# Attention scores made with keys on partitions, seeded with the row minimum, instead of turned probabilities

## What is computed

```
xn  = layernorm(x)
qg, k, v = split(xn @ w_qkv.T);  q, gate = split(qg)
q, k = rope(layernorm(q)), rope(layernorm(k))
scores = q k^T / sqrt(128), causal                  # 16 heads, 2048 x 2048
out = softmax(scores) @ v                           # a key head serves 4 query heads
out = (out * sigmoid(gate)) @ w_o.T
moe = sum over the 2 best experts of p_e * (relu(xn @ w_fc[e])**2 @ w_proj[e])
result = x + out + moe
```

## Time and profile before

| | |
|---|---|
| time, median of 3 runs | 1535.22 us (1534.33 to 1535.95) |
| span of the profiled execution | 1534.4 us, 29715 instructions |
| busy TensorE | 1501.5 us (98%) |
| busy TensorE weight loads | 1380.6 us (90%) |
| busy VectorE | 1304.1 us (85%) |
| busy ScalarE | 1152.4 us (75%) |
| busy GpSimd | 364.7 us (24%) |

### The profile page before, as it was taken

The page is one execution under the profiler, slowest core; times in us unless marked ns, Lnnn a source line. Parts: engine busy times, 40 slices in busy tenths (PEclk is TensorE's granted clock), DMA queues, the critical chain, the costliest instruction groups (busy, mean ns, idle before and its releaser), DMA issues.

```text
span 1534.4 us, 29715 instructions
## 1 busy us (share of the span) xinstructions
PE 1501.5 (98%) x10589; PEld 1380.6 (90%) x10589; DVE 1304.1 (85%) x3037; ACT 1152.4 (75%) x3017; POOL 364.7 (24%) x502
## 2 busy tenths in 40 slices
PE   5999999999999999999999999999999999999998
PEld 3889999999989999999998999999999899999998
DVE  8999888888998888788799888877879888887788
ACT  4777776778887778777878777777787877768765
POOL 6545434420322111111042211111104221011010
PEclk8999999999999999999999999999999999999999
DMA  5411011011121111111111110111022211001013
GB/s 175 163 38 46 28 43 51 30 53 49 60 60 49 35 42 49 39 39 39 59 59 59 40 49 12 49 39 39 20 74 63 60 49 42 18 22 31 9 50 124
DMA packets 45124, 78.82 MB, mean 51 GB/s; under 512 B 4784, under 2 KB 30896, under 8 KB 44784
## 3 DMA queue, kind: packets, MB, share of 16 engines
q1 hardware_dynamic: 41232, 66.65, 14.2%
q0 software_dynamic: 3744, 10.26, 1.9%
HBM read 58.25 MB, written 24.72 MB: 54 GB/s over the span
## 4 chain that ended last, share of the span: by engine, by line
PE 86%; DVE 8%; ACT 3%; issue 2%; DMA 1%; POOL 1%; SPq 0%; DVEq 0%; ACTq 0%; POOLq 0%
PE bank L1392 45%; PE o_bank L1392 22%; PE pt_bank L1467 14%; PE bank L1445 2%; PE bank L1488 2%; DVE t_same L1266 1%; DVE pT_lo L1316 1%; ACT probs L1017 1%; DVE bank L1299 1%; DVE t_same L1262 1%; ACT pT_hi L1036 1%; DVE neg_chunk_max L1302 1%; DVE sumsq L1234 1%; DVE t_same L1250 1%; PE bank L1509 1%
## 5 line engine op out<-in xcount | busy, mean ns | idle before, releaser
L1017 ACT ACTIVATE probs<-bank,neg_max 128x512 f32<-128x512 f32 (+3 forms) x640 | 400.0, 635 | 100.8 <-DVE neg_max L1309 61.5
L1316 DVE TENSOR_TENSOR pT_lo<-pt_bank,pT_hi 128x512 fp32r<-128x512 f32 (+1 forms) x576 | 369.5, 655 | 87.4 <-ACT pT_hi L1036 82.9
L1036 ACT ACTIVATE pT_hi<-pt_bank 128x512 fp32r<-128x512 f32 (+1 forms) x576 | 326.7, 579 | 119.7 <-PE o_bank L1392 59.3
L1392 PE MATMUL o_bank<-pT_hi,v_hi 128*128 128x256 f32 x1088 | 331.8, 305 | 0.4 <-DVE pT_lo L1316 0.3
L1467 PE MATMUL pt_bank<-ident_rows,probs 128*128 128x128 f32 x2176 | 313.3, 273 | 2.5 <-DVE pT_lo L1316 1.5
L1392 PE MATMUL o_bank<-pT_hi,v_lo 128*128 128x256 f32 x1088 | 307.2, 282 | 0.0
L1392 PE MATMUL o_bank<-pT_lo,v_hi 128*128 128x256 f32 x1088 | 306.6, 282 | 0.0
L1302 DVE TENSOR_REDUCE neg_chunk_max<-bank 128x1 f32<-128x512 f32 (+1 forms) x384 | 244.8, 651 | 58.7 <-PE bank L1392 58.1
L1467 PEld LDWEIGHTS pt_bank<-ident_rows,probs 128*128 128x128 f32 x2176 | 252.1, 140 | 25.2 <-DVE pT_lo L1316 3.8
L1392 PE MATMUL bank<-kT_hi,qT_hi 128*128 128x512 f32 (+3 forms) x640 | 242.7, 379 | 0.7 <-ACT probs L1017 0.6
L1392 PE MATMUL bank<-kT_hi,qT_lo 128*128 128x512 f32 (+3 forms) x640 | 231.2, 361 | 0.0
(11 more groups left out here) (167 smaller groups left out, 2852.1 us busy)
## 6 DMA issues: line engine op xcount, KB each, us to landing
norm_rows<-kept_tables SPq DMA_DIRECT2D x24, 384.0 KB, 3.1
made_tables<-kept_tables SPq DMA_DIRECT2D x24, 384.0 KB, 3.0
kept_tables<-made_tables SPq DMA_DIRECT2D x16, 384.0 KB, 2.5
rows<-xs SPq DMA_DIRECT2D x23, 258.0 KB, 2.7
expert_raw<-in_w_fc SPq DMA_DIRECT2D x23, 256.0 KB, 3.0
expert_raw<-in_w_proj SPq DMA_DIRECT2D x23, 256.0 KB, 2.7
xs<-in_x_fill SPq DMA_DIRECT2D x11, 516.0 KB, 5.4
w_raw<-in_w_in SPq DMA_DIRECT2D x7, 640.0 KB, 4.2
```

What stands on the lines that cost most here:

```text
L1017: act.activation(probs[:, u, h % 2, first:first + width], bank("scores", g, t, h, c)[:, 0:width], ACT.Exp, bias=neg_max[:, u, h % 2:h % 2 ...
L1036: act.activation(pT_hi[:, n % PT_RING, 0:width], pt_bank[n % 2][:, 0:width], ACT.Copy)\
L1316: dve.tensor_tensor(pT_lo[:, n % PT_RING, 0:width], pt_bank[n % 2][:, 0:width], pT_hi[:, n % PT_RING, 0:width].bitcast(F32), ALU.subtract) ...
L1392: ins = pe.matmul(out_ap, s, m, start=(start and done == 1), stop=(stop and done == last))
```

## The change

The scores are now made with the keys on partitions, so that the exponentials come out as the value product needs them and nothing is turned.

- A softmax needs the row extreme before the exponential. It now comes from a one-pass product of the hi parts alone: `A` (PE, one matmul in place of three, queries on partitions), then `max` as before, and `min` over the chunks where there are several. The 128 x 4 result `row_min` is stored to memory (`mu_store`) and loaded back spread over all partitions (`mu_load`) as `min_rows`, 128 x 512: query and head in the columns.
- For each block j of 128 keys: `seed` (ScalarE, Copy with scale -1) writes the negated `min_rows`, or for the diagonal block `masked_min` (made by GpSimd, `masked`), into one of two banks `st_bank`. `st` adds the three-pass product of key block and 512 query columns on top (no matmul of it starts a group). `exp` writes `pT_raw` in SBUF, a ring of three; `p_hi` and `p_lo` now read `pT_raw`, and `pv` takes 512 columns at once. One `bits` step at the start puts the two banks into the state in which matmuls add.
- The accumulator of `exp` can't give row sums now. GpSimd adds the blocks up element by element, `psum`, one instruction of 128 x 512 for each block but the first of a tile (484 in all), into `lane_sum`. `SUMT` turns it, `sums` reduces it on VectorE, and the inverse goes out to memory and back (`inv_store`, `inv_load`); only in the last tile it is turned by TensorE (`INVB`).
- The gate projection is made turned, 128 features by 512 tokens, for four tiles at once (`G`, 64 steps as before). `gate_scale` and `GT` are gone. `og0` (VectorE) multiplies gate and `o_bank` in place of `o_take` and `og`; the product with the inverse sum, `og`, is GpSimd's (63 instructions of 128 x 512).
- The seven other banks: two for `st_bank` (before: `pt_bank`), five general ones, now free for any step. `BEGIN` and `DUE` have new values. qT, oT are now double buffers.

The core of the diff:

```diff
+ST_BANKS = 2
+RAW_RING = 3
@@ program_steps
-                    add("pe S", ("scores", g, t, h, c), SCORE_US[w], [("k_lo", g, t)],
-                        b + DUE["scores"])
+                    add("pe A", ("A", g, t, h, c), APPROX_US[w], [("k_hi", g, t)], at)
+            for j in range(t + 1):
...
+                add("act seed", ("seed", g, t, j), 0.48, [("mu_load", g, t), ("masked", g, t) if j == t else None,
+                    back("exp", ST_BANKS), ("bits",)], at + DUE["seed"])
+                add("pe S", ("st", g, t, j), 0.695, [("seed", g, t, j), ("k_lo", g, t)], at)
+                freed = [back("p_lo", RAW_RING)]
...
+                    freed.append(("psum", g0, t0, 1 if t0 and not j0 else j0))
+                add("act S", ("exp", g, t, j), 0.5, [("st", g, t, j)] + freed, at + DUE["exp"])
+                add("act PT", ("p_hi", g, t, j), 0.5, [("exp", g, t, j), back("pv", PT_RING)], at + DUE["p_hi"])
+                add("dve PT", ("p_lo", g, t, j), 0.6, [("p_hi", g, t, j)], at + DUE["p_lo"])
@@ GpSimd
+                    else:
+                        w.wait_ge(summed, number[step] - 1)
+                        pool.tensor_tensor(total, pT_raw[:, (m - 1) % RAW_RING] if j == 1 else total, pT_raw[:, m % RAW_RING],
+                                           ALU.add).then_inc(summed, 1)
+                elif kind == "og":
...
+                    pool.tensor_tensor(oT[:, t % 2], oT[:, t % 2], inv_rows[:, t % 2], ALU.mult).then_inc(og_done, 1)
@@ ScalarE
-                    act.activation(probs[:, u, h % 2, first:first + width],
-                                   bank("scores", g, t, h, c)[:, 0:width], ACT.Exp, bias=neg_max[:, u, h % 2:h % 2 + 1], scale=-1.0,
-                                   accum_out=chunk_sum[:, t % 2, h, c:c + 1]).then_inc(exp_done, 1)
+                    if m >= RAW_RING:
+
+                        w.wait_ge(pt_lo_done, m - RAW_RING + 1)
+                        w.wait_ge(summed, raw_freed(m - RAW_RING))
+                    act.activation(pT_raw[:, m % RAW_RING], st_bank[m % ST_BANKS][:], ACT.Exp, scale=-1.0).then_inc(exp_done, 1)
@@ VectorE
-                    dve.tensor_tensor(pT_lo[:, n % PT_RING, 0:width], pt_bank[n % 2][:, 0:width],
-                                      pT_hi[:, n % PT_RING, 0:width].bitcast(F32), ALU.subtract).then_inc(pt_lo_done, 1)
+                    dve.tensor_tensor(pT_lo[:, m % PT_RING], pT_raw[:, m % RAW_RING], pT_hi[:, m % PT_RING].bitcast(F32),
+                                      ALU.subtract).then_inc(pt_lo_done, 1)
@@ TensorE
+                    w.wait_ge(seeded, m + 1)
+                    three(st_bank[m % ST_BANKS][:], [(kT_hi[:, keys], kT_lo[:, keys])], [(qT_hi[:, t % 2], qT_lo[:, t % 2])],
+                          start=False, seeded_bank=True).then_inc(st_filled, 1)
```

583 lines of the change are left out of this document (316 added, 267 removed), and 27 rows, old and new, of the table BEGIN.

## The result

The changed kernel takes **2312.05 us** (median, 2309.49 to 2314.26), the kernel before 1534.80 beside it: 1.506 times as long, 95% interval 1.504 to 1.509. The forecast was 1587 us, with a range up to 1690. The direction was right, the size was not: 725 us are missing from the sum. The kernels of experiments 1 and 8 were timed four times, the others once; executions of one kernel lie within 6 us of each other.

The account below looks back on a forecast made before the run. TensorE's stream of products bound the kernel before; after the change VectorE would, with 1320 us of own load, 220 of port waits and idle of 9, 7 and 30, span 1586: forecast 1587 us, range 1425 to 1690.

Parts of the forecast that it names:

- between ... I allow 2%, 30 us: VectorE idle between start and end of the span, also for short tiles where the minimum goes through memory: 30 us.
- The wait at the port: VectorE instructions with two SBUF inputs wait for GpSimd's SBUF-reading products: 0.36 us for each of 611, 220 us.
- its own load: VectorE's busy time without port waits: 1304 + 13, about 1320 us, 93% of TensorE's 1413.
- the likeliest case: VectorE held up at the port: 1587 us, own range 1520 to 1680, chance 0.57.
- how long does VectorE wait for one GpSimd product?: Port step: at least 0, at most 1.06 us; by chance order 0.32 + 0.04 = 0.36 us.
- 46 us of idle: Idle on top of VectorE's 1540: 9 us at the start, 7 at the end, 30 between; span 1586.
- the floor of 1413: TensorE alone after a net 121 us less: 1534 - 121 = 1413 us, the ceiling of the gain.
- Ports meet rarely: Rival: block sums fall beside VectorE's reductions and gaps, waits under 0.1 us each; 1425 us, chance 0.23.
- Two banks: Rival: seed, products, exponential through two score banks cost 0.2 us on each of 364 blocks; about 1490 us, chance 0.11.
- GpSimd behind: Rival: late GpSimd sums hold everybody through the ring of three `pT_raw`, 2 us a tile; 1715 us, chance 0.09.
- Doesn't keep the products together: Rival: 512-column value products no cheaper than two of 256, TensorE losing only 9 us; inside the range, no chance given.
- The marks: Signs of being right: `pT_lo` 0.9 us or more, VectorE over 95%, TensorE under 93%, GpSimd's 512-wide products 1.4 or more.

Follow-up runs that it names:

- experiment 1: Changed kernel without either trip through memory: TensorE turns spread row minima and inverse sums, VectorE multiplies by the inverse; 1836.99 us, 1.197 times the kernel before.
- Experiment 8: Kernel of experiment 1 with the exponential written over the scores in PSUM, both parts split from there, GpSimd summing the high parts, three score banks; 1805.06 us.
- experiment 4: Changed kernel with both stores as 128 rows of 16 bytes in place of 512 single floats, both trips and the order kept; 1848.12 us.
- experiment 9: Kernel of Experiment 8 with each GpSimd block sum replaced by three fills of together 1.3 us; 1617.80 us.
- Experiments 7 and 12: 7: kernel of experiment 1, each GpSimd block sum replaced by three fills, 1588.50 us; 12: kernel before, 512 times four GpSimd fills added, 1640.28 us.
- the nearest, at 1577: Kernel of experiment 1 with each GpSimd block sum replaced by one fill of the same 512 columns; 1576.51 us.

## Why the prediction was wrong

**The trips through memory: the step that failed.** The prediction put them into "between ... I allow 2%, 30 us", with "a transfer of 384 KB lands after 3.0 us; here two in a row, behind others on SyncE". The forecast charged the trip to the short tiles; the trace has the seeds wait for it 52 times, up to 15.9 us, in all parts of the span. Two things were wrong. The row is of a transfer in long pieces, and the new stores are in pieces of 4 bytes, which the diff says in so many words (`allow_slow_non_contiguous=True`, "h q -> q h"); they land after 9.1 us. And the wait was not multiplied: the two trips take 9.1 + 4.6 + 9.0 + 4.8 = 27.5 us for each of 64 tiles, of which the span has 36.1 each, and SyncE stands 15.8 of them, with everything behind it. No row of before has such a store, so the term needed both bounds, as the port got, and had one. Measured: 464 us by experiment 4 (475 by experiment 1) in place of part of 30. That alone is 60% of the 777, and added to the forecast it goes beyond the range.

**The wait at the port: right mechanism, a term too small.** Forecast 0.36 us for each of 611 products, 220 us on VectorE. Experiment 4 has the changed kernel's instructions and order without the long stores, and VectorE is busy 1705 us there against its own load of 1320 as forecast, so 385, or 0.63 each. (That load is borne out within 2%: 1387 less 43 for the moved products, 1344, in experiment 9, where little is held.) In the changed kernel itself, where everything stands more, it is 1625 less 1320, 305. The 385 are within the bounds of 0 and 648, but their 0.63 is above the 0.5 a product at which the likeliest case ended. What failed is "how long does VectorE wait for one GpSimd product?": I asked it for each product of GpSimd, took chance order, and let at most one instruction of VectorE wait, once. Two rows of experiment 1 say otherwise. Products of the rope come five in a row just when GpSimd, after `rstd`, works off its sums without a gap, and one may wait for two. On the rope's 320 products alone VectorE spent 107 us more in experiment 1 (121.1 + 75.4 against 89.8), on the low parts about 140.

**What follows the wait.** I turned VectorE's load into time by adding 46 us of idle. In experiment 4 it was 141 (1846 less 1705): 1320 + 385 + 141 = 1846, where I had 1320 + 220 + 46 = 1586. These 260 us and the 464 of the stores are the whole miss, and 1848 lies outside the range already, so the second error alone would have failed the forecast too. That the idle comes by way of the rope is in part argued: TensorE waits there 131 us for `t_same`, VectorE's own idle is spread over many waits. Experiment 8 speaks for it from the other side: 131 us less of VectorE's low parts gave 32, or 61 with banks and order made equal.

The Trainium skill, SBUF — State Buffer, Who interferes with whom, was cited for this contention. It says that a VectorE instruction with two SBUF inputs contends with a GpSimd instruction that reads SBUF, not with one that only writes it. Experiments 7 and 12 agree (386 and 349 ns beside fills, 668 and 454 beside reading). Who comes second is blocked in full by that section; read as one instruction's wait at most, as the prediction read it, this is too little, by the 3343 ns above.

**TensorE.** The pitch of the 512-column value product was to be 0.232; in experiment 1 three follow from 1600.39 to 1600.86, 0.235 each. With the port out of the way its busy time is 1481 us against 1501 before. That is a gain of 21 where I had 121 and the turns of minima and inverse sums take some 56 back; busy time includes the overlap of products that wait, so the rest isn't settled. No run came near the floor of 1413; the nearest, at 1577, has TensorE at 94% and VectorE at 90%.

**The clock.** In the changed kernel the mean granted clock is 0.853 of 2.4 GHz with TensorE busy 71%, without trips 0.952 with 86%, with the fills 0.996 with 93%, as in the kernel before. Its products got longer with it: the first score product of a block means 483 ns in the changed kernel and 435 in experiment 1. The prediction had no word on it. I take it for a consequence of TensorE's standing; what the lower clock adds to the time no run separates.

**GpSimd and ScalarE.** GpSimd's 512-column product was to be 1.23 us and takes 1.27 undisturbed; busy 1115 forecast, 1272 measured. ScalarE 1210 forecast, 1242 measured.

**The rivals.** *Ports meet rarely* is refuted by the low part's 933 ns. *Two banks*: TensorE does wait 341 us for the seeds (its weight loads 388), as that rival would have it, but the seeds wait for the minima from memory, not for `exp`; without the trips TensorE's wait for seeds is 23 us. *GpSimd behind*: `exp` waits 77 us for scores, 55 for `pT_lo` and only 14 for `lane_sum`. *Doesn't keep the products together*: it does.

**The marks.** `pT_lo` at 0.9 and more, GpSimd at 1.4 and more, TensorE under 93%: all three came true, and they don't tell 1587 from 2312. Two marks failed and told of the trips: VectorE over 95% came out as 70%, and TensorE's longest waits end not with `pT_lo` or reductions but with the seeds. Group 0 was to lose most: its first 16 tiles end 184 us later (the first product of the rope with the tables of group 1 starts at 572.6 in place of 388.2), about a quarter of the 777, so no more than its share.

## What to carry to other kernels

These small stores were priced by their pieces, not their bytes: look at which dimension lies contiguous at both ends, and if the trace has no transfer of that form, bound it from both sides, multiply by the number of trips, and ask what stands behind the wait in its queue. When work is added to a planned kernel for an experiment, look whether the order stayed the same. Where two engines share a port, count the short instructions that come in a row, and ask who waits for the last of them; the sum over all instructions is only the first part of the time. And to tell a port from a queue, replace one engine's work by fills of the same length.

## What the runs showed of the hardware

- A store of 2 KB in 512 pieces of 4 bytes lands after 9.1 us, in 128 pieces of 16 bytes after 1.4. While the former run, a load of 384 KB takes 5.2 us in place of 3.0.
- A VectorE instruction with two inputs in SBUF, 0.34 us long, was held up to 3.0 us by a row of GpSimd instructions that read SBUF. With one of its inputs in PSUM it isn't held (681 ns in the mean, the longest of 544 takes 694), and fills by GpSimd hold it little or not (349 and 386 ns).
